# Side jobs dealt anew over eight slots, q computed once and its halves exchanged by transfers, v taken from k's job

## The chip, the core and the metric

The kernel runs on one core of one Trainium2 chip. The time is the device time of one execution in microseconds (us). TensorE is called PE in the profile, VectorE DVE, ScalarE ACT, GpSimd POOL, SyncE SP (SPq is its queue, which issues the transfers here).

## What is computed

A block of a transformer on x of shape (16, 512, 128), all in float32:

```python
xn = layernorm(x)
# attention, 16 heads of 8, 4 kv heads
q = (xn @ Wqa @ Wqb).reshape(b, s, 16, 8)
kv = (xn @ Wkva @ Wkvb).reshape(b, s, 4, 8, 2)
k, v = kv[..., 0], kv[..., 1]
q, k = rope(q), rope(k)          # pairs (2i, 2i+1) of a head's 8 numbers are rotated
k, v = repeat(k, 4), repeat(v, 4)
w = softmax(causal(q @ k.T * 8 ** -0.5))
attn = (w @ v) @ Wout + bout
# feed-forward with blocks of 16 quantized to FP4, 352 hidden
gate, up = fp4_linear(xn, w_gate), fp4_linear(xn, w_up)
ffn = fp4_linear(silu(gate) * up, w_down)
out = x + attn + ffn
```

## The kernel before

The work is a software pipeline over the 16 batches. Iteration T runs from -3 to 16; `Step.has(off)` says whether batch T+off exists. In iteration T the kernel computes the exponentials and weighted sums of batch T, the row maxima of batch T+1, the hidden layer's gate and up of T+1, the projections q, k, v and the quantization of xn of T+2, the statistics and normalization of x of T+3, and normalizes and stores the output of T-1.

An iteration has 8 slots (one for each pair of heads). On TensorE a slot is, in program order (`iteration`, L1125): six `max_tile` (scores for the maxima, three PSUM banks `max_ps`) and five `exp_tile` (scores for the exponentials, two banks `exp_ps`) in turn, with side jobs at three points: point 0 after exp tile 1, point 1 after exp tile 3, point 2 after max tile 5, and then `weighted_sums`, half of a kv head (L1057). The table `MISC` (L56) gives the side jobs of each slot and point as (job, bank, batch offset). A side job writes one of the two banks `misc_ps`, and waits until the bank's previous job has been read (`misc_wait`). Jobs: gate/up f (matmuls of token tile f), xnT, xqT, onT, ot0, ot1, hqT (transposes of normalized x, quantized x, normalized output, sums, quantized hidden layer), q and qrot (the projection and the same with each pair's columns swapped), kk (k and swapped k, four column groups each), v, mrow (the rows of maxima), out0 and out1.

Each engine carries out its own list in order. ScalarE (L968): after each exp its side read (th, up_half, the copies of the transposes) and `extra`: casts of q, k, x_mag (slot 0), h_mag (`H_POWERS`, L67), `normalize_x` in slot 5. VectorE (L715): six `reduce_tile` in a slot (the maxima, L662) with its own jobs between them: q_cos, q_sin, k_cos, k_sin, `gated`, `hidden_max`, `normalize`, `magnitudes`, `output`. GpSimd (L525): `causal` (masks P, four instructions for a kv head), `quantize` parts 0 to 3 of h and xq, `hidden`, q_rope, k_rope and their splits, the statistics. SP (L410): the transfers; `place_max` waits for ScalarE's m_row and puts the maxima's rows into Q; q_split and k_split go to scratch in DRAM and come back as Q and K.

Rope before is `q_rope = q_cos + q_sin`, q_cos from the q job and q_sin from the qrot job, each times a table.

Of the kernel before, what the change touches and what calls it, by code (L numbers as in the profile page):

```python
# [9 lines left out]
ALU = mybir.AluOpType  # L10
# [24 lines left out]
WRITE_Q, WRITE_K = 3, NT  # L35
LOAD_K, LOAD_Q, COPY_K = 6, 2, 2
# [88 lines left out]
def build(nc, x, wqaT, wkvaT, wqb, wkvb, wout, bout, wgate, wup, wdown, cosq, sinq, cosk, sink,  # L125
          mask_q, mask_k, out):
    ctx = ExitStack()
    with ctx:
# [46 lines left out]
        q_sin = sb("q_sin", [128, S])  # L175
        q_rope = sb("q_rope", [128, S])
# [6 lines left out]
        k_split = sb("k_split", [128, 3, 128], BF16)  # L183
        v_stage = sb("v_stage", [128, NT, KVH * D])
# [61 lines left out]
        xn_done = sem("xn_done")  # L246
        q_pool = sem("q_pool")
# [65 lines left out]
        def _(sp):  # L313
            sp.dma_start(x_in[:, :, :], x[0].rearrange("(c p) e -> p c e", p=128)).then_inc(x_loaded, 16)
            for dst, src in (
                (wqaT_sb[:, :], wqaT), (wkvaT_sb[:, :], wkvaT), (wqb_sb[:, :], wqb), (wkvb_sb[:, :], wkvb),
            ):
                sp.dma_start(dst, src).then_inc(factors_in, 16)
            for dst, src in (
                (cosq_sb[:, :], cosq), (sinq_sb[:, :], sinq), (cosk_sb[:, :], cosk), (sink_sb[:, :], sink),  # L320
            ):
                sp.dma_start(dst, src).then_inc(tables_in, 16)
# [24 lines left out]
            for half in range(2):  # L347
                r = HALF * half + MROW
                for i in range(2):
# [5 lines left out]
                    dst = bass.AP(tensor=q_scr[i].tensor, offset=NSLOT * E * S + half * D * NPAIR * S,  # L355
                                  ap=[[NPAIR * S, D], [128, NPAIR * NT], [1, 128]])
# [97 lines left out]
        def _(pool):  # L454
# [70 lines left out]
            def iteration(T):  # L525
# [6 lines left out]
                split_rest(T, 0, 1)  # L532
                hidden(T, 0)
# [7 lines left out]
                if T.has(0):  # L541
                    quantize(T, 0, 0, *hs)
# [13 lines left out]
                if T.has(2):  # L556
                    T.misc_wait(pool, misc_read, "q")
                    T.misc_wait(pool, misc_read, "qrot")
                    nc.gpsimd.tensor_tensor(q_rope[:, :], q_cos[:, :], q_sin[:, :], ALU.add).then_inc(q_pool, 1)
                    T.wait(pool, k_muls, 1, 2, 1)  # L560
                    T.misc_wait(pool, misc_read, "kk")
# [44 lines left out]
        def _(dve):  # L606
# [80 lines left out]
            def normalize(T, off, g):  # L687
# [27 lines left out]
            def iteration(T):  # L715
# [4 lines left out]

                reduces(0, 0, 1)
# [7 lines left out]
                reduces(0, 4)  # L729
                if T.has(2):  # L730
                    T.wait(dve, x_powers, 1, 2, 1)
                    magnitudes(lambda s, n: T.wait(dve, s, 2, 2, n), x_mag[:, :], x_mags)
                reduces(0, 5)
                first = T.t0 == FIRST_T + 1
                if first:
                    weight_scales()

                reduces(1, 0, 1)
                if T.has(2):
# [12 lines left out]
                reduces(2, 0, 1, 2)  # L752
                if T.has(2):
                    T.misc_wait(dve, misc_filled, "qrot")
                    nc.vector.tensor_tensor(q_sin[:, :], misc_ps[1][:, :], sinq_sb[:, :], ALU.mult).then_inc(misc_read[1], 1)
                reduces(2, 3)
                hidden_max(T, 1)
                reduces(2, 4)
                if T.has(2):

                    T.wait(dve, k_pool, 3, 1, 1)
                    T.misc_wait(dve, misc_filled, "kk")
                    nc.vector.tensor_tensor(k_cos[:, :], misc_ps[0][:, 0:128], cosk_sb[:, :], ALU.mult).then_inc(k_muls, 1)
                    nc.vector.tensor_tensor(k_sin[:, :], misc_ps[0][:, 128:256], sink_sb[:, :], ALU.mult).then_inc(misc_read[0], 1)
                reduces(2, 5)
# [5 lines left out]
                normalize(T, -1, 1)  # L771
                reduces(3, 1)
                if T.has(3):
                    T.wait(dve, x_loaded, 16, 3, 16)

                    T.wait(dve, var_done, 2, 2, 2)
# [4 lines left out]
                reduces(3, 3)
                if T.has(3):
                    for c in range(NT):
                        T.wait(dve, bn_done, NT, 3, c + 1)
                        dve.sem_inc(dve_marks, 1)
                        nc.vector.bn_aggr(bn_mv[:, c, :], bn_raw[:, c, :]).then_inc(mv_done, 1)
                reduces(3, 4)
# [8 lines left out]
                if T.has(0):  # L796
                    T.wait(dve, h_powers, NT, 0, NT)
                    magnitudes(lambda s, n: T.wait(dve, s, 2, 0, n), h_mag[:, :], h_mags)
                reduces(4, 1, 2)
# [22 lines left out]
                reduces(6, 3)  # L822
                reduces(6, 4, 5)
# [396 lines left out]
```

## Time and profile before

| | before |
|---|---|
| median of 3 runs | 816.93 us (815.31 to 818.28) |
| profiled execution | 814.38 us, of which the span from first to last instruction is 812.6 us |
| PE busy | 742.4 us, 91% of the span |
| DVE busy | 636.3 us, 78% |
| POOL busy | 606.1 us, 75% |
| ACT busy | 554.2 us, 68% |
| mean granted clock of TensorE | 0.985 |

Busy time is what an engine spends in instructions; a slot's time is read off as the distance of two starts. "x4" after a line of the timeline means four instructions merged, and "[0.27 <-DVE ...]" idle time before them and who ended it. A matmul's shown end lies a little behind the start of the next one, as they are pipelined. Some matmul records are missing from the trace.

### The profile page before, as it was taken

What the parts mean: (1) busy time and instruction counts of PE and PEld (TensorE: products, weight loads), DVE (VectorE), ACT (ScalarE), POOL (GpSimd) and SP (SyncE); (2) the same over time, 40 slices, a digit from 0 to 9 for tenths busy, and PEclk for the clock granted to TensorE, in tenths of its full rate; (3) what the DMA queues carried; (4) which work ended last, traced back from release to release, by engine and by line L of the source; (5) the groups of instructions that cost most, each with busy time, mean ns of one, the idle gap of its engine ahead of it and who ended that gap; (6) DMA issues with size and microseconds to landing.
All of it is one profiled execution on the core that took longest, in us unless ns stands there. A gap on an engine that the chain in (4) does not pass through costs nothing.

```text
span 812.6 us, 18664 instructions
## 1 busy us (share of the span) xinstructions
PE 742.4 (91%) x6641; PEld 465.3 (57%) x6733; DVE 636.3 (78%) x1394; ACT 554.2 (68%) x1170; POOL 606.1 (75%) x707
## 2 busy tenths in 40 slices
PE   2376999999999999999999999999999999999986
PEld 1233555665656566665656566665656566665544
DVE  5569888888788888888788888888788888877511
ACT  1212677777777777777777777777777777677672
POOL 5533697878788797878788797878788797856662
PEclk9977899999999999999999999999999999999999
DMA  4423232141414233241414232141414232240000
GB/s 113 122 55 103 55 97 59 57 114 47 100 33 111 54 97 73 66 105 46 101 34 110 55 103 68 57 114 46 102 35 107 54 94 63 59 99 3 28 8 20
DMA packets 66518, 58.24 MB, mean 72 GB/s; under 512 B 17554, under 2 KB 56434, under 8 KB 66426
## 3 DMA queue, kind: packets, MB, share of 16 engines
q1 hardware_dynamic: 66426, 57.04, 27.4%
q8 instruction: 54, 0.88, 0.5%
q14 instruction: 38, 0.31, 0.1%
HBM read 31.81 MB, written 18.61 MB: 62 GB/s over the span
## 4 chain that ended last, share of the span: by engine, by line
PE 73%; DVE 8%; ACT 6%; POOL 5%; issue 3%; SPq 2%; DMA 2%; another core or an unknown queue 0%; POOLq 0%; DVEq 0%; ACTq 0%
PE pv_ps L1057 18%; PE max_ps L1021 12%; PE exp_ps L1036 11%; PE misc_ps L1073 6%; PE max_ps L1022 6%; PE misc_ps L1122 5%; DVE neg_max L662 4%; PE misc_ps L1081 3%; PE misc_ps L1100 3%; ACT P L854 2%; PE misc_ps L1120 2%; PE misc_ps L1110 2%; PE misc_ps L1090 1%; POOL P L478 1%; PE misc_ps L1077 1%
## 5 line engine op out<-in xcount | busy, mean ns | idle before, releaser
L662 DVE TENSOR_REDUCE neg_max<-max_ps 128x1 f32<-128x512 f32 (+3 forms) x768 | 433.4, 594 | 110.3 <-PE max_ps L1022 108.7
L854 ACT ACTIVATE P<-exp_ps 128x512 f32<-128x512 f32 x512 | 293.5, 596 | 176.8 <-remote 95.7
L1021 PE MATMUL max_ps<-K,Q 128*128 128x384 bf16 (+2 forms) x768 | 199.7, 279 | 24.6 <-DMA Kd<-K 10.9
L1036 PE MATMUL exp_ps<-Q,K 128*128 128x384 bf16 (+3 forms) x932 | 208.4, 292 | 7.5 <-ACT P L854 6.0
L1022 PE MATMUL max_ps<-Kd,Q 128*128 128x128 bf16 x1024 | 190.7, 221 | 1.5 <-DVE neg_max L662 1.5
L478 POOL TENSOR_SCALAR_AFFINE_SELECT P<-P 128x512 f32<-128x512 f32 x256 | 161.6, 667 | 32.6 <-ACT P L857 32.6
L1057 PE MATMUL pv_ps<-P,V 128*32 128x512 f32 (+3 forms) x2048 | 164.2, 439 | 1.2 <-POOL P L478 0.8
L1021 PEld LDWEIGHTS max_ps<-K,Q 128*128 128x128 bf16 x768 | 75.2, 100 | 96.0 <-DVE neg_max L662 42.7
L1022 PEld LDWEIGHTS max_ps<-Kd,Q 128*128 128x128 bf16 x1024 | 99.4, 99 | 42.6 <-issue 22.8
L510 POOL TENSOR_TENSOR h<-gate_sb,up_half 128x352 f32<-128x352 f32 x64 | 59.6, 932 | 62.4 <-DVE gate_sb L675 62.3
L1036 PEld LDWEIGHTS exp_ps<-Q,K 128*128 128x128 bf16 x1024 | 82.3, 98 | 37.0 <-ACT P L854 14.2
L1057 PEld LDWEIGHTS pv_ps<-P,V 128*32 128x32 f32 x2048 | 53.7, 109 | 80.5 <-issue 70.8
L1073 PE MATMUL misc_ps<-wguT,xqT 128*128 128x352 f32 x256 | 94.0, 481 | 3.9 <-DVE o_norm L698 3.7
L857 ACT ACTIVATE P<-exp_ps 128x512 f32<-128x512 f32 x128 | 77.6, 606 | 0.4 <-PE exp_ps L1036 0.4
L1073 PEld LDWEIGHTS misc_ps<-wguT,xqT 128*128 128x128 f32 x256 | 47.0, 195 | 26.3 <-DVE o_norm L698 11.6
L1122 PE MATMUL misc_ps<-wdT,hqT 128*128 128x128 f32 (+1 forms) x384 | 53.3, 275 | 0.0
L1122 PEld LDWEIGHTS misc_ps<-wdT,hqT 128*128 128x128 f32 (+1 forms) x384 | 48.0, 192 | 0.0
L491 POOL TENSOR_TENSOR h<-h,h_mag 128x1408 f32<-128x1408 f32 x16 | 45.9, 2868 | 1.3
L488 POOL TENSOR_TENSOR h<-h,h_mag 128x1408 f32<-128x1408 f32 x16 | 45.8, 2862 | 0.0
L485 POOL TENSOR_TENSOR h<-h,h_inv 128x1408 f32<-128x1408 f32 x16 | 41.4, 2590 | 0.0
L494 POOL TENSOR_TENSOR h<-h,h_scale 128x1408 f32<-128x1408 f32 x16 | 41.4, 2589 | 0.0
L924 ACT ACTIVATE xn<-x_in,shift,rstd 128x128 f32<-128x128 f32 x64 | 30.5, 487 | 15.2 <-POOL shift L523 15.2
(113 smaller groups left out, 1024.0 us busy)
## 6 DMA issues: line engine op xcount, KB each, us to landing
Q<-q_scr SPq DMA_DIRECT2D x64, 224.0 KB
q_scr<-q_split SPq DMA_DIRECT2D x16, 384.0 KB, 2.6
Kd<-K SPq DMA_DIRECT2D x64, 96.0 KB
x_in<-x SPq DMA_DIRECT2D x16, 256.0 KB, 5.3
q_scr<-q_split SPq DMA_DIRECT2D x16, 256.0 KB, 2.9
x_res<-x SPq DMA_DIRECT2D x16, 256.0 KB, 5.8
out<-y SPq DMA_DIRECT2D x32, 128.0 KB, 3.1
K<-k_scr SPq DMA_DIRECT2D x64, 48.0 KB
```

The source lines that it names most:

```text
L478: nc.gpsimd.affine_select(out=diag, in_=diag, compare_op=ALU.is_ge, fill=0.0, base=0, pattern=[[0, GH], [1, 128]], channel_multiplier=-1). ...
L491: nc.gpsimd.tensor_tensor(t, t, mag[:, :], ALU.subtract).then_inc(quant, 1)
L510: nc.gpsimd.tensor_tensor(h[T.par(1)][:, f * F:(f + 1) * F], gate_sb[f % 2][:, :], up_half[f % 2][:, :], ALU.mult).then_inc(h_made, 1)
L662: nc.vector.tensor_reduce(neg_max[:, pr // 4, i, heads[0]:heads[0] + len(heads), pr % 4], max_ps[r % 3][:, 0:len(heads) * n].rearrange("p ...
L854: nc.scalar.activation(P[g % 2][:, hh + r % 2, col:col + 512], ps[:, :], ACT.Exp, scale=SCALE).then_inc(exp_done, 1)
L857: nc.scalar.activation(P[g % 2][:, hh:hh + 2, P_COL[2]:P_COL[2] + 256], ps[:, :].rearrange("p (h q) -> p h q", h=2), ACT.Exp, scale=SCALE) ...
L1021: nc.tensor.matmul(ps[:, col:col + d], Qt, Kt[:, half, g, 0:d], start=True, stop=True)
L1022: last = nc.tensor.matmul(ps[:, col + d:col + n], Qt, Kd[:, half, g, d:n], start=True, stop=True)
L1036: last = nc.tensor.matmul(exp_ps[n % 2][:, col:col + width], K[par][:, half, pr // 2, kb * 128:(kb + 1) * 128], Q[par][:, pr, kb * 128:S], ...
L1057: last = nc.tensor.matmul(pv_ps[32 * j:32 * j + 32, kb * 128:S], V[T.par(off)][:, kb, g, :], P[g % 2][:, j, P_COL[kb]:P_COL[kb] + width], ...
L1073: last = nc.tensor.matmul(ps[:, 0:F], xqT[T.par(1)][:, tok[f]], wguT[:, int(job[0] == "u"), :], start=True, stop=True)
L1122: last = nc.tensor.matmul(ps[:, tok[n]], hqT[0:cn, k, tok[c]], wdT[0:cn, k, :], start=False, stop=(k == 2))
```

## The change

Side jobs. The new table (with the batch offsets as in the old one):

```python
MISC = [
    [[("gate0", 0, 1), ("up0", 1, 1)], [], [("q", 1, 2)]],
    [[], [("gate1", 0, 1), ("up1", 1, 1)], [("ot0", 1, -1)]],
    [[("mrow1", 0, 0)], [], [("ot1", 1, -1), ("kkv", 0, 2)]],
    [[("gate2", 0, 1), ("up2", 1, 1)], [("v", 1, 2)], [("xqT", 0, 2)]],
    [[("gate3", 0, 1), ("up3", 1, 1)], [("onT", 1, -1)], []],
    [[], [("out0", 0, -1)], []],
    [[("out1", 0, -1)], [("mrow0", 1, 1)], []],
    [[("xnT", 1, 3)], [("hqT0", 0, 0), ("hqT1", 1, 0)], [("hqT2", 0, 0)]],
]
H_POWERS = [(1, 0), (1, 1), (1, 2), (2, 2)]
```

xnT moves from slot 0 to slot 7 of the iteration before, ot0 (and the division of its sums) from slot 7 to slots 1 and 2 of the next iteration, xqT from slot 5 to 3, three h_mag casts of ScalarE to slot 1 and one to slot 2.

q: qrot is gone. The tables and q are laid out by dimension (16 rows for each of the 8 numbers), VectorE makes q_cos and q_sin both from the q job, eight transfers of 16 rows exchange q_sin's pairs, and GpSimd subtracts:

```diff
+            def swap_q(T):
+                T.misc_wait(sp, misc_read, "q")
+                T.wait(sp, q_pool, 3, 1, 1)
+                for d in range(D):
+                    r, o = H * d, H * (d ^ 1)
+                    sp.dma_start(q_swap[r:r + H, :], q_sin[o:o + H, :]).then_inc(q_swapped, 16)
...
                     sp.dma_start(x_res[:, :, :], x[T.batch(0)].rearrange("(c p) e -> p c e", p=128)).then_inc(x_res_loaded, 16)
+                if T.has(2):
+                    swap_q(T)
+                if T.has(0):
                     place_max(T, 0, 1)
...
-                    nc.gpsimd.tensor_tensor(q_rope[:, :], q_cos[:, :], q_sin[:, :], ALU.add).then_inc(q_pool, 1)
+                    T.wait(pool, q_muls, 1, 2, 1)
+                    T.wait(pool, q_swapped, 16 * SWAP_Q, 2, 16 * SWAP_Q)
+                    nc.gpsimd.tensor_tensor(q_rope[:, :], q_cos[:, :], q_swap[:, :], ALU.subtract).then_inc(q_pool, 1)
```

v: it is computed transposed as a third set of the k job, copied to SBUF by VectorE, and transposed back:

```diff
-                elif job == "kk":
-                    for n in range(2):
-                        w = proj[:, 2 * E + n * KVH * D:2 * E + (n + 1) * KVH * D]
+                elif job == "kkv":
+                    for n in range(3):
+                        w = proj[:, E + n * KVH * D:E + (n + 1) * KVH * D]
                         for c in range(NT):
                             last = nc.tensor.matmul(ps[32 * c:32 * c + 32, n * 128:(n + 1) * 128], w, xnT[:, tok[c]], start=True, stop=True)
                 elif job == "v":
-                    for c in range(NT):
-                        last = nc.tensor.matmul(ps[:, 32 * c:32 * c + 32], xnT[:, tok[c]],
-                                                proj[:, 2 * E + 2 * KVH * D:], start=True, stop=True)
+                    T.misc_wait(pe, misc_read, "kkv")
+                    last = nc.tensor.transpose(ps[:, 0:128], vT[:, :], ident[:, :])
```

GpSimd: part 0 of h's quantization goes ahead of hidden(0), part 3 ahead of causal(2). VectorE's list in the new order, by slot (r0 to r5 are the reductions):

```
0: r0 r1 scales(h) r2 r3 gated0 r4 r5 q_cos
1: r0 q_sin r1 magnitudes(x) r2 r3 r4 gated1 r5
2: r0 normalize0 r1 r2 r3 r4 r5 normalize1 k_cos k_sin vT
3: r0 magnitudes(h) r1 r2 gated2 r3 r4 v_stage r5
4: r0 bn_stats r1 bn_aggr r2 gated3 r3 r4 r5
5: r0 r1 hidden_max0 r2 r3 hidden_max1 r4 output0 r5
6: r0 r1 x_max r2 output1 r3 hidden_max2 r4 r5
7: r0 r1 scales(x) r2 r3 hidden_max3 r4 r5
```

## Rows read from the trace of the kernel before

**Rows 1.** Busy time by stretch (T=7): length, PE, PEld, DVE, ACT, POOL, clock, DMA, GB/s

```profile
401.46:447.16 45.70, 44.87 (x418) 28.69 (x421) 38.72 (x86) 34.30 (x73) 37.48 (x44) 1.00 0.29 76
```

**Rows 2.** Timeline of TensorE, T=7: start us, us, engine, line, operation, tiles, count

```profile
404.59 0.66 PE L1077 MATMUL misc_ps<-ident,xn 128*128 128x128 f32 x4
...
406.95 0.34 PE L1021 MATMUL max_ps<-K,Q 128*128 128x384 bf16 x1
...
407.82 1.02 PE L1081 MATMUL misc_ps<-xnT,proj 128*128 128x512 f32 x2
408.68 0.27 PE L1021 MATMUL max_ps<-K,Q 128*128 128x256 bf16 x1
...
412.55 0.34 PE L1021 MATMUL max_ps<-K,Q 128*128 128x384 bf16 x1
...
415.67 0.64 PE L1087 MATMUL misc_ps<-xnT,proj 128*32 128x128 f32 x16
...
418.56 0.34 PE L1021 MATMUL max_ps<-K,Q 128*128 128x384 bf16 x1
...
421.92 1.03 PE L1090 MATMUL misc_ps<-proj,xnT 128*128 128x32 f32 x8
...
424.65 0.34 PE L1021 MATMUL max_ps<-K,Q 128*128 128x384 bf16 x1
...
428.21 0.23 PE L1021 MATMUL max_ps<-K,Q 128*128 128x128 bf16 x1
...
430.11 0.34 PE L1021 MATMUL max_ps<-K,Q 128*128 128x384 bf16 x1
...
435.90 0.34 PE L1021 MATMUL max_ps<-K,Q 128*128 128x384 bf16 x1
```

**Rows 3.** Timeline of TensorE, T=14, slots 0 to 2

```profile
721.11 0.34 PE L1021 MATMUL max_ps<-K,Q 128*128 128x384 bf16 x1
...
724.41 0.39 PE L1036 MATMUL exp_ps<-Q,K 128*128 128x256 bf16 x2
...
726.06 0.34 PE L1021 MATMUL max_ps<-K,Q 128*128 128x384 bf16 x1
...
727.35 0.39 PE L1036 MATMUL exp_ps<-Q,K 128*128 128x384 bf16 x2
...
729.96 1.28 PE L1057 MATMUL pv_ps<-P,V 128*32 128x384 f32 x16
731.17 0.34 PE L1021 MATMUL max_ps<-K,Q 128*128 128x384 bf16 x1
...
736.46 0.34 PE L1021 MATMUL max_ps<-K,Q 128*128 128x384 bf16 x1
```

**Rows 4.** Timeline of ScalarE, T=7, slots 0 and 2

```profile
404.06 0.47 ACT L893 ACTIVATE up_half<-misc_ps 128x352 f32<-128x352 f32 x1
404.41 1.10 ACT L854 ACTIVATE P<-exp_ps 128x512 f32<-128x512 f32 x2
...
415.88 0.49 ACT L965 ACTIVATE h_mag<-h 128x352 bf16<-128x352 f32 x1
```

**Rows 5.** Timeline of VectorE, T=7, slot 4

```profile
428.54 0.51 DVE L675 SCALAR_TENSOR_TENSOR gate_sb<-th,misc_ps 128x352 f32<-128x352 f32 x1
```

**Rows 6.** Timeline of SP's queue, T=7: start us, us, line, transfer, count

```profile
415.24 2.56 SPq L408 DMA_DIRECT2D Q<-m_row  x4
```

**Rows 7.** Transfers by line: count, KB each, median us from issue to landing

```profile
q_scr<-q_split SPq DMA_DIRECT2D x16, 384.0 KB, 2.6
...
k_scr<-k_split SPq DMA_DIRECT2D x64, 24.0 KB, 1.6
```

**Rows 8.** Timeline of all engines in the fill, T=-2 and the start of T=-1

```profile
22.64 1.26 POOL L559 TENSOR_TENSOR q_rope<-q_cos,q_sin 128x512 f32<-128x512 f32 x1 [0.46 <-DVE q_sin L755]
...
25.13 0.41 SPq L439 DMA_DIRECT2D x_in<-x  x1
...
43.96 0.48 PE L1021 MATMUL max_ps<-K,Q 128*128 128x384 bf16 x1 [8.88 <-DMA Kd<-K]
```

More of the change, by code:

```diff
@@ L532, in iteration @@
                 split_rest(T, 0, 1)
+                if T.has(0):
+                    quantize(T, 0, 0, *hs)
                 hidden(T, 0)
@@ L728, in iteration @@
                 gated(T, 0)
[L729 to L734, printed above, removed]
+                reduces(0, 4, 5)
                 if first:
                     weight_scales()
-                reduces(1, 0, 1)
                 if T.has(2):
@@ L770, in iteration @@
                 reduces(3, 0)
[L771 to L776, printed above, removed]
-                    for c in range(NT):
-                        nc.vector.bn_stats(bn_raw[:, c, :], x_in[:, c, :]).then_inc(bn_done, 1)
-                reduces(3, 2)
-                gated(T, 2)
[L781 to L787, printed above, removed]
+                if T.has(0):
+                    T.wait(dve, h_powers, NT, 0, NT)
+                    magnitudes(lambda s, n: T.wait(dve, s, 2, 0, n), h_mag[:, :], h_mags)
+                reduces(3, 1, 2)
+                gated(T, 2)
+                reduces(3, 3, 4)
                 if T.has(2):
@@ L795, in iteration @@
                 reduces(4, 0)
[L796 to L799, printed above, removed]
+                if T.has(3):
+                    T.wait(dve, x_loaded, 16, 3, 16)
+                    T.wait(dve, var_done, 2, 2, 2)
+                    for c in range(NT):
+                        nc.vector.bn_stats(bn_raw[:, c, :], x_in[:, c, :]).then_inc(bn_done, 1)
+                reduces(4, 1)
+                if T.has(3):
+                    for c in range(NT):
+                        T.wait(dve, bn_done, NT, 3, c + 1)
+                        dve.sem_inc(dve_marks, 1)
+                        nc.vector.bn_aggr(bn_mv[:, c, :], bn_raw[:, c, :]).then_inc(mv_done, 1)
+                reduces(4, 2)
                 gated(T, 3)
-                reduces(4, 3)
-                hidden_max(T, 2)
-                reduces(4, 4, 5)
+                reduces(4, 3, 4, 5)
                 if first:
                     store_weights()
-                reduces(5, 0, 1, 2)
+                reduces(5, 0, 1)
+                hidden_max(T, 0)
+                reduces(5, 2, 3)
+                hidden_max(T, 1)
+                reduces(5, 4)
                 output(T, 0)
-                reduces(5, 3, 4)
-                hidden_max(T, 3)
                 reduces(5, 5)
@@ L1074, in misc_job @@
                 elif job == "xnT":
-                    T.wait(pe, xn_done, NT, 2, NT)
+                    T.wait(pe, xn_done, NT, off, NT)
                     for c in range(NT):
                         last = nc.tensor.transpose(ps[:, tok[c]], xn[:, c, :], ident[:, :])
-                elif job in ("q", "qrot"):
-                    T.misc_wait(pe, misc_read, "xnT")
-                    c0 = E * int(job == "qrot")
-                    last = nc.tensor.matmul(ps[:, :], proj[:, c0:c0 + E], xnT[:, :], start=True, stop=True)
-                elif job == "kk":
-                    for n in range(2):
-                        w = proj[:, 2 * E + n * KVH * D:2 * E + (n + 1) * KVH * D]
+                elif job == "q":
+                    T.prev().misc_wait(pe, misc_read, "xnT")
+                    last = nc.tensor.matmul(ps[:, :], proj[:, 0:E], xnT[:, :], start=True, stop=True)
+                elif job == "kkv":
+                    for n in range(3):
+                        w = proj[:, E + n * KVH * D:E + (n + 1) * KVH * D]
                         for c in range(NT):
```

101 lines of the change are left out of this document (53 added, 48 removed), and 6 rows, old and new, of the table MISC.

## Prediction

> **What bounds the kernel now.** I read the busy time by stretch first. One iteration T handles the attention of batch T, the maxima of T+1 and the projections of T+2. In T=7, TensorE is busy 44.87 of 45.70 us at its full clock (granted clock 1.00, the 2.4 GHz level), VectorE 38.72, ScalarE 34.30, GpSimd 37.48 [rows 1]. The timeline of TensorE gives the slots: each starts with the first `max_tile` matmul, so T=7, from 401.46 to 447.16, has slots of 5.49, 5.60, 6.01, 6.09, 5.46 and 5.79 us, and 11.26 for slots 6 and 7 together [rows 1, 2]. T=14 starts at 721.11 [rows 3]; the seven iterations from 401.46 take 45.66 each, so the loop is regular and what one iteration gains or loses counts some 15 times.
>
> But TensorE's queue is in order, and it stands still as soon as the next tile has no bank. Three couplings matter. An exp tile n+2 needs exp tile n read by ScalarE (two banks). A max tile n+3 needs n reduced by VectorE. A side job needs the previous job of its misc bank read. So the question for each slot is what fills TensorE while ScalarE works, not only what TensorE has to do.
>
> T=14 shows that: it has no batch T+2, so xnT, q, qrot, kk, v are absent. Its slot 1 has nothing at point 0, as in the new plan. It lasts 5.11 us (726.06 to 731.17), where 5.60 less the q job (0.86, from 407.82 to 408.68) would be 4.74: exp tile 2 starts only 1.29 us after the slot's start [rows 2, 3]. Of 0.86 us taken off, 0.37 came back as waiting.
>
> **Matmul work.** Removed per iteration: qrot, like q 0.86; v 1.03 less the 0.16 by which a shown end lies behind the next start, 0.87. Added: a third set of four matmuls in kkv, half of the 0.57 that kk takes (0.64 less overlap), 0.29; and one transpose of vT (four take 0.66 less 0.17 = 0.49 after a wait; I take 0.44 for four without one, an estimate), a quarter of that and some start, 0.17 [rows 2]. Net -1.27.
>
> **Slots, one by one, in the new plan** (S is the slot's start).
>
> Slot 0 (gate0/up0; q at point 2). T=14's slot 0, without xnT, is 4.95. There exp tile 4 starts at S+3.30 [rows 3]. In T=7 ScalarE also casts x_mag, so its third exp starts at S+2.95, ends at S+3.55 [rows 4], and TensorE can follow 0.06 later, at S+3.61 (the 0.06: up_half starts at 404.06 and lasts 0.47, xnT starts at 404.59 [rows 2, 4]). xnT used to fill that time; q now comes behind it. 4.95 + 0.31 + 0.86 = 6.12 (before 5.49).
>
> Slot 1 (nothing; gate1/up1; ot0). Base 5.11. Three h_mag casts move here, each 0.49 long; ScalarE's instructions overlap by 0.1, so two exps take 1.10 and not 1.20, and a cast costs 0.39 [rows 4]. ScalarE: first exp at S+0.64, then four exp steps of 0.49, three casts of 0.39, th 0.35, up_half 0.46, some 0.04 less in all by the overlaps: bank 1 free at S+4.54, TensorE at S+4.60. In T=14 the weighted sums start at S+3.90 [rows 3], with 0.10 of weight load before them, so ot0 could have started at S+3.80. 5.11 + 0.80 + 0.49 (four transposes after such a wait) = 6.40 (5.60). Were ScalarE not late it would be 5.55.
>
> Slot 2 (mrow1; nothing; ot1, kkv). T=14's slot 2 has just mrow1 and ot1 and lasts 5.29 [rows 3]. kkv adds 0.57 + 0.29 + 0.09 = 0.95: 6.24 (6.01).
>
> Slot 3 (gate2/up2; v; xqT). The h magnitudes (two VectorE instructions) move here from slot 4. In T=7's slot 4 they hold max tile 4 until S+3.56 (428.21), behind onT [rows 2]; now behind the small v job. xqT then waits until `gated` has read gate2: S+3.89 plus 0.51 is S+4.40 [rows 5]. 4.46 + 0.49 + 0.10 + 1.21 (the weighted sums, 729.96 to 731.17 [rows 3]) = 6.26 (6.09; the wait of up2 on `normalize` goes, since that is moved ahead of slot 3).
>
> Slot 4 (gate3/up3; onT) loses the magnitudes: 5.46 - 0.31 = 5.15 (an estimate: max tile 4 right behind onT instead of at 428.21). Slot 5 (nothing; out0) loses xqT, 0.44, and gets the wait of an empty point 0, 5.11 - 4.74 = 0.37, and a normalize_x between the exps that costs as an h_mag cast does, 0.39: 6.11 (5.79). Slots 6 and 7: xnT alone at point 0, the hqT jobs stay; 11.3 (11.26).
>
> Sum 6.12 + 6.40 + 6.24 + 6.26 + 5.15 + 6.11 + 11.3 = 47.58, against 45.70: **+1.85 us an iteration**, rounded. Bounds: +2.6 (GpSimd late in slot 6 by 0.5, slots 6 and 7 as much as slot 2) and +0.9 (ot0 finds its bank free, and slot 4 lends its 0.3 to slot 3).
>
> **GpSimd.** h part 3 goes ahead of causal(2), 2.6 us before it. h part 0 moves ahead of hidden(0): both have slack. Counting its chain from `gated` in slot 3, the first two of causal(2) end within 0.1 us of when TensorE wants them in slot 6. I take 0, bound 0.5. V and vT copies: VectorE gets 0.2 us more in 38.72 of 45.70, hidden at slot ends; uncovered it would be 0.2.
>
> **SP and the swap.** `swap_q` issues eight transfers, then `place_max(T, 0, 1)` waits behind it. Four transfers from `place_max` took 2.56 us to issue, so eight take 5.1; landings have medians of 1.6 (24 KB) and 2.6 (384 KB), so 2 for these 32 KB [rows 6, 7]. q_sin is there at S0+7.8, the last issue ends at S0+12.9, and the last landing is at about 15; q_rope comes up on GpSimd at S0+16.5, and its cast on ScalarE at S0+19.9. In the steady loop the swap is hidden, with some 4 us; uncovered, it would delay ScalarE in slot 3.
>
> In the fill it is not hidden. SP is held by the constants until 25.13, when it issues the x load of 0.41 [rows 8]; then come eight issues, 5.1, and 2 of landing: q_rope at 32.6 rather than 22.64 [rows 8]. Bounds: issues of 0.4 each give 30.8, landings of twice as long 34.6. GpSimd and ScalarE are in order, so k_rope, both splits and the cast of the weights are behind it, and the first max tile, which idled 8.88 us until 43.96 for its K [rows 8], moves with them. **+9.5 us** (+6 to +12).
>
> By the Trainium skill, *DMA: Bandwidth & Descriptors*, "Rules for kernel authors", transfers under 64 KB are mostly overhead and should be coalesced; these are 32 KB each. Its section on the anatomy of one DMA gives about 2.0 us fixed for one on another path; paid one after another, eight of them would be an estimated 16 us instead of 7. No row of before shows these transfers.
>
> **Ends.** T=0 as the loop, +1.8 (the ends are estimates by the same steps). T=14 has ot0 and the casts in slot 1 but less in slots 3, 4 and 7: +0.8. T=15 and T=16: +1.5.
>
> Sum: 812.6 of span + 1.8 around it = 814.4; + 9.5 + 1.8 + 13 x 1.85 (24.0) + 0.8 + 1.5 = 852.0. The median of before (816.9) is 2.5 above its profiled run, so some 854.
>
> **Rivals.**
> 1. *ScalarE late, fill longer* (forecast): 854, own range 841 to 868. For it: T=14. Chance 0.70.
> 2. *TensorE's work counts in full*: the waits are covered by other tiles; -1.27 x 16 = -20, fill +9.5: about 806. For it: 44.87 of 45.70 busy. Against: T=14's slot 1 saved 0.49 of 0.86. It decides if exp tile 2 starts before S+1.1 in the new slot 1. Chance 0.08.
> 3. *Half*: ot0 finds bank 1 free and slot 3's waits overlap (+0.9 down to 0), or the fill moves by 3 only: 822 to 841. Chance 0.13.
> 4. *The swap lands late in the loop*: eight transfers one after another put q_rope at S0+24, 4 us behind its place, some 2 to 4 us of TensorE per iteration: 880 to 915. The 2 us each are my landing estimate of above. (It is the Trainium skill's rule, *DMA: Bandwidth & Descriptors*, "Rules for kernel authors", as a mechanism of this kernel.) Against: SP idles ahead of q_sin, and transfers overlap elsewhere. Chance 0.07. An outcome within 0.3% of before (about what a measurement of this kernel can tell from no change) needs a gain in the loop that just cancels the fill: 0.02.
>
> Range 832 to 870: the forecast's range, half of rival 3 and the unknown bounds. Faster 0.08, same 0.02, slower 0.90.
>
> **What would show it.** After: slots of about 6.1, 6.4, 6.2, 6.3, 5.15, 6.1; TensorE idle by "ACT P" (exp) in slots 0, 1, 2, 5; ot0 starting 0.06 after up_half in slot 1; the first max tile near 53 us; q_rope never idle on its transfer in the loop. It is wrong if slot 1 stays below 5.7, if the first max tile stays near 44, or if TensorE waits in slot 6 for GpSimd by more than 0.5.

## The result, and the profile after

The changed kernel takes 836.81 us (median, 836.56 to 837.29); the kernel before, run on the same chip beside it, 816.84 (815.31 to 818.28). The ratio is 1.0248, 95% interval 1.0225 to 1.0270: slower, as forecast, but by 20 us and not by 37.

| | before | after |
|---|---|---|
| span of the profiled execution | 812.6 us | 835.6 us |
| PE busy | 742.4 us, 91% | 738.6 us, 88% |
| DVE busy | 636.3 us, 78% | 621.6 us, 74% |
| POOL busy | 606.1 us, 75% | 600.0 us, 72% |
| ACT busy | 554.2 us, 68% | 544.8 us, 65% |
| first max tile starts | 43.96 | 50.66 |
| an iteration of the loop (T=7) | 45.70 | 46.81 |

Every engine has less to do and the kernel is slower. Below, "before" is the kernel before and "after" the changed one; the fill is the stretch up to T=0, in which the pipeline is not yet full. The busy time by stretch, for the eight slots of T=7 in the kernel after (columns as in [rows 1]), with the sum of the iteration last:

```profile
413.02:419.19 6.17, 5.77 (x48) 3.08 (x45) 5.33 (x11) 3.99 (x9) 5.05 (x6) 1.00 0.52 151
419.19:425.61 6.42, 5.75 (x50) 3.13 (x47) 4.76 (x10) 4.41 (x10) 3.58 (x5) 1.00 0.21 52
425.61:431.56 5.95, 5.39 (x75) 3.20 (x71) 5.21 (x13) 3.83 (x8) 5.18 (x10) 1.00 0.08 18
431.56:437.35 5.79, 5.64 (x52) 3.31 (x48) 4.74 (x10) 4.97 (x11) 3.87 (x5) 1.00 0.00 0
437.35:442.49 5.14, 5.14 (x51) 3.26 (x48) 4.61 (x15) 4.17 (x10) 4.82 (x12) 1.00 0.51 167
442.49:448.59 6.10, 5.70 (x59) 3.82 (x56) 4.42 (x9) 4.18 (x9) 6.02 (x3) 1.00 0.33 88
448.59:454.31 5.72, 5.72 (x63) 4.10 (x59) 4.58 (x9) 3.59 (x7) 5.64 (x7) 1.00 0.48 133
454.31:459.83 5.52, 5.46 (x59) 3.78 (x55) 4.20 (x11) 4.49 (x9) 2.86 (x4) 1.00 0.18 48
sum 46.81, PE 44.57 PEld 27.69 DVE 37.86 ACT 33.63 POOL 37.02; mean PE 5.57 PEld 3.46 DVE 4.73 ACT 4.20 POOL 4.63
```

It answers [rows 1]: the gap between an iteration's length and PE's busy time was 0.83 us before and is 2.24 now, and it lies in slots 0, 1, 2 and 5. (Before, the eight slots were 5.49, 5.60, 6.01, 6.09, 5.46, 5.79, 5.72 and 5.54, read from the starts of their first max tiles; the same slot differs by up to 0.02 from one iteration to the next. About six matmul records an iteration are missing before, x932 against x1024 in the rows below, so its gap is, if anything, read too large.) The groups of the costliest instructions say who ended the idle time, first of after, then of before (busy, mean ns | idle before, releaser):

```profile
L1056 PE MATMUL exp_ps<-Q,K 128*128 128x512 bf16 (+3 forms) x1024 | 244.0, 301 | 33.7 <-ACT P L877 28.0
```

```profile
L1036 PE MATMUL exp_ps<-Q,K 128*128 128x384 bf16 (+3 forms) x932 | 208.4, 292 | 7.5 <-ACT P L854 6.0 <-issue 0.6
```

Exp tiles waited 28.0 us in all for ScalarE to read their bank, against 6.0. The chain that ended last turned the same way, of after and then of before:

```profile
PE 54%; ACT 24%; issue 8%; DVE 5%; SPq 4%; POOL 3%; DMA 2%; ACTq 0%; POOLq 0%; DVEq 0%
```

```profile
PE 73%; DVE 8%; ACT 6%; POOL 5%; issue 3%; SPq 2%; DMA 2%; another core or an unknown queue 0%; POOLq 0%; DVEq 0%; ACTq 0%
```

Where it sat in the new slot 1, by the timelines of ScalarE and TensorE of after:

```profile
420.33 0.49 ACT L985 ACTIVATE h_mag<-h 128x352 bf16<-128x352 f32 x1
...
421.19 0.50 ACT L985 ACTIVATE h_mag<-h 128x352 bf16<-128x352 f32 x1
...
422.06 0.51 ACT L985 ACTIVATE h_mag<-h 128x352 bf16<-128x352 f32 x1
...
423.26 0.49 ACT L913 ACTIVATE up_half<-misc_ps 128x352 f32<-128x352 f32 x1
...
423.81 0.66 PE L1128 MATMUL misc_ps<-ident,oT 128*128 128x128 f32 x4 [0.26 <-ACT up_half L913]
```

Three casts stand ahead of up_half; it ends at 423.75, and ot0 starts 0.06 later.

The fill, by the timeline of the queue of SP, GpSimd and TensorE; it answers [rows 8]:

```profile
25.52 0.40 SPq L461 DMA_DIRECT2D x_in<-x  x1
25.96 5.02 SPq L427 DMA_DIRECT2D q_swap<-q_sin  x8
32.46 1.26 POOL L581 TENSOR_TENSOR q_rope<-q_cos,q_swap 128x512 f32<-128x512 f32 x1 [6.77 <-DMA q_swap<-q_sin]
...
44.91 0.73 SPq L396 DMA_DIRECT2D Q<-q_scr  x2
...
50.66 0.48 PE L1041 MATMUL max_ps<-K,Q 128*128 128x384 bf16 x1 [2.60 <-DMA Kd<-K]
```

The same load of Q, and the first max tile, in before:

```profile
35.07 1.66 SPq L385 DMA_DIRECT2D Q<-q_scr  x2
```

The swap came as forecast, and the 9.8 us it costs q_rope did not all reach the first max tile: 6.7 did. The two transfers that load Q took 0.73 us to issue instead of 1.66, which the forecast did not have.

### The profile page after: what moved, and what is told of

The parts are those of the page before. It is cut to its first block, busy times and chain, and to the rows that moved or that the text cites. A ratio compares the mean times of both kernels' runs of the same rounds, so it can differ in the third digit from the quotient of the medians.

```text
span 835.6 us, 18869 instructions
## 1 busy us (share of the span) xinstructions
PE 738.6 (88%) x6717; PEld 449.4 (54%) x6717; DVE 621.6 (74%) x1411; ACT 544.8 (65%) x1170; POOL 600.0 (72%) x707
## 4 chain that ended last, share of the span: by engine, by line
PE 54%; ACT 24%; issue 8%; DVE 5%; SPq 4%; POOL 3%; DMA 2%; ACTq 0%; POOLq 0%; DVEq 0%
PE pv_ps L1077 18%; ACT P L877 11%; PE exp_ps L1056 10%; PE max_ps L1041 6%; PE misc_ps L1140 5%; DVE neg_max L683 3%; PE max_ps L1042 3%; PE misc_ps L1093 3%; ACT up_half L913 2%; PE misc_ps L1128 2%; ACT h_mag L985 2%; PE misc_ps L1138 2%; ACT th L900 2%; PE misc_ps L1100 1%; PE misc_ps L1118 1%
## 5 line engine op out<-in xcount | busy, mean ns | idle before, releaser
L683 DVE TENSOR_REDUCE neg_max<-max_ps 128x1 f32<-128x512 f32 (+3 forms) x768 | 429.1, 593 | 137.1 <-PE max_ps L1042 136.9
L1056 PE MATMUL exp_ps<-Q,K 128*128 128x512 bf16 (+3 forms) x1024 | 244.0, 301 | 33.7 <-ACT P L877 28.0
L500 POOL TENSOR_SCALAR_AFFINE_SELECT P<-P 128x512 f32<-128x512 f32 x256 | 153.4, 635 | 37.4 <-ACT P L880 37.4
L1056 PEld LDWEIGHTS exp_ps<-Q,K 128*128 128x128 bf16 x1024 | 77.7, 98 | 86.0 <-ACT P L877 65.5
L1093 PE MATMUL misc_ps<-wguT,xqT 128*128 128x352 f32 x256 | 88.6, 469 | 0.4 <-DVE vT L786 0.4
L510 POOL TENSOR_TENSOR xq<-xq,x_mag 128x512 f32<-128x512 f32 x16 | 18.5, 1155 | 44.5 <-DVE x_mag L645 44.5
L620 POOL TENSOR_TENSOR xq<-xn,x_inv 128x512 f32<-128x512 f32 x16 | 16.9, 1058 | 37.3 <-DVE x_inv L636 37.3
```

The costliest lines, as they stand in the source:

```text
L500: nc.gpsimd.affine_select(out=diag, in_=diag, compare_op=ALU.is_ge, fill=0.0, base=0, pattern=[[0, GH], [1, 128]], channel_multiplier=-1). ...
L510: nc.gpsimd.tensor_tensor(t, t, mag[:, :], ALU.add).then_inc(quant, 1)
L683: nc.vector.tensor_reduce(neg_max[:, pr // 4, i, heads[0]:heads[0] + len(heads), pr % 4], max_ps[r % 3][:, 0:len(heads) * n].rearrange("p ...
L1056: last = nc.tensor.matmul(exp_ps[n % 2][:, col:col + width], K[par][:, half, pr // 2, kb * 128:(kb + 1) * 128], Q[par][:, pr, kb * 128:S], ...
L1093: last = nc.tensor.matmul(ps[:, 0:F], xqT[T.par(1)][:, tok[f]], wguT[:, int(job[0] == "u"), :], start=True, stop=True)
```

## The experiments

The theory: (A) TensorE loses where it waits for ScalarE with no side job to fill the wait, so what counts is where side jobs and casts stand. (B) The fill pays the swap. Against them: that the arithmetic itself (q once, v in k's job) costs, or that a transfer does. First I put the two pieces of arithmetic in the old deal (the old table of side jobs), together and apart. Each ratio is to the kernel before on the same chip; medians of runs on different chips are less comparable.

**Both in the old deal.** The deal, casts and orders are those of before; the jobs and the rope are those of after:

```diff
-    [[("mrow1", 0, 0), ("qrot", 1, 2)], [("kk", 0, 2)], [("ot1", 1, -1)]],
+    [[("mrow1", 0, 0)], [("kkv", 0, 2)], [("ot1", 1, -1)]],
```

> q once with the exchange, and v in k's job, but side jobs, casts and VectorE's and GpSimd's order as before. Theory A (the new deal of side jobs costs the time: ScalarE's waits at empty points and behind the casts): the loop gets shorter than before's 45.68 us, by about 0.5 in slot 2 and 0.4 in slot 3 less 0.2 of waiting for q_sin in slot 1, so 44.9 to 45.1 an iteration; the fill is 5 us longer; in all 808 to 813 profiled. Rival B (q once, the exchange and v in k are themselves what costs): the loop stays at 46.5 or above, 830 or more.

Measured: 820.46 us, ratio 1.0076 (1.0061 to 1.0092); first max tile at 50.35, iteration 45.83. Neither theory's number came: 44.9 to 45.1 had been expected by A, 46.5 or more by B. Slots 2, 3 and 4 are shorter (5.83, 5.65 and 5.31), but slot 1 is 5.90 and slot 7 is 6.14 instead of 5.54; the two runs below say why. Of the 20 us some 6 belong to the arithmetic and its fill, and the rest to the new deal, with the orders of VectorE and GpSimd that came with it. In the profiled execution, 7.9 longer than before's, T=1 starts 4.7 us later than before, T=1 to T=13 add 1.6, and the last stretch adds 1.6.

**q once alone**, without kkv and vT:

> Only q once with the exchange, deal as before. Theory A: loop 45.68 - 0.5 (qrot was partly cover for ScalarE in slot 2, of its 0.86 only 0.5 come back) + 0.2 (up1 waits until q_sin has read the bank) = 45.4; fill +5; in all 814 to 817 profiled, level with before. Rival B: loop 46 or more, 825 or more.

Measured: 820.72 us, ratio 1.0077 (1.0061 to 1.0094). First max tile at 49.89, iteration 45.57, a little more than the 45.4 expected, and a time 3 us above the 814 to 817 (T=1 starts 3.5 us later than before, the loop gives back 1.3; behind T=14 the profiled execution had a granted clock of 0.90 instead of 1.00 and took 3.5 longer). The product that left slot 2 gave 0.40 us there (6.01 to 5.61), but slot 1 grew by 0.30 (5.61 to 5.91): both q products are now made by VectorE from bank 1 ahead of up1. The timeline of VectorE and of TensorE in this kernel:

```profile
411.84 0.69 DVE L764 TENSOR_TENSOR q_cos<-misc_ps,cosq_sb 128x512 f32<-128x512 f32 x1 [0.29 <-PE misc_ps L1100]
412.45 0.68 DVE L767 TENSOR_TENSOR q_sin<-misc_ps,sinq_sb 128x512 f32<-128x512 f32 x1
```

```profile
412.34 1.71 PE L1093 MATMUL misc_ps<-wguT,xqT 128*128 128x352 f32 x4
```

The gate and up pair takes 1.71 us from start to end, against 1.40 in the same slot of after; up1 waits until q_sin has been made, at 413.13. Removing 0.86 us of matmuls per iteration bought 0.1.

**v in k's job alone**:

```diff
-                    for n in range(2):
+                    for n in range(3):
...
+                    nc.vector.tensor_copy(vT[:, :], misc_ps[0][:, 256:384]).then_inc(misc_read[0], 1)
...
+                    last = nc.tensor.transpose(ps[:, 0:128], vT[:, :], ident[:, :])
```

> Only v taken from k's job and transposed back, deal as before. Theory A: slot 2 +0.1, slot 3 -0.7 + 0.26 (exp tile 4 then waits for ScalarE), so loop -0.3 an iteration, no change in the fill: 808 to 811 profiled. Rival B (copy and transpose on the path): level or slower, 814 or more.

Measured: 819.60 us, ratio 1.0060 (1.0045 to 1.0075), iteration 45.89: a miss, since I had expected a gain. Slots 2, 3 and 4 went from 6.01, 6.09, 5.45 to 6.23, 5.65, 5.31, which is the gain I had expected (-0.36). Slot 7, where nothing had been touched, went from 5.53 to 6.11 and took more than that back, a net loss of 2.2 us from T=1 to T=14 (3.5 more lie behind T=14 in the profiled execution, again at a clock of 0.90 instead of 1.00). Its third transpose of h waits for `normalize` (L698), and `normalize` is late behind a tiny instruction. Timelines of this kernel, VectorE, GpSimd and TensorE:

```profile
398.58 0.84 DVE L611 TENSOR_SCALAR x_scale<-x_max 128x32 f32<-128x32 f32 x1
```

```profile
398.11 1.27 POOL L592 TENSOR_TENSOR x_bias<-x_res,bout_sb 128x512 f32<-128x512 f32 x1
```

```profile
401.26 0.64 PE L1102 MATMUL misc_ps<-ident,h 128*96 128x128 f32 x4 [0.44 <-DVE o_norm L698]
```

And the same pair in before:

```profile
443.25 0.27 DVE L611 TENSOR_SCALAR x_scale<-x_max 128x32 f32<-128x32 f32 x1
```

```profile
442.22 1.27 POOL L592 TENSOR_TENSOR x_bias<-x_res,bout_sb 128x512 f32<-128x512 f32 x1
```

The same 32 numbers a partition took 0.84 us here and 0.27 there. In both, x_scale ends 0.03 to 0.04 us after x_bias: 399.42 after 399.38, and 443.52 after 443.49. So x_scale seemed to be held until GpSimd's instruction had ended; with TensorE 0.4 us quicker in slots 2 to 4, VectorE came to it 0.6 us earlier in x_bias's run.

**x_bias moved.** To test that, GpSimd carries out x_bias behind the scaling of xq, its next instruction, instead of ahead of it; the rest is as in the run before.

```diff
-                    nc.gpsimd.tensor_tensor(x_bias[:, :, :], x_res[:, :, :],
...
                     nc.gpsimd.tensor_tensor(blocks(xq[:, :]), blocks(xn[:, :, :].rearrange("p c e -> p (c e)")),
...
+                    nc.gpsimd.tensor_tensor(x_bias[:, :, :], x_res[:, :, :],
```

> v in k's job alone (as in v_only), and on GpSimd x_bias is put behind the xq scaling instead of ahead of it. Theory: VectorE's small x_scale instruction (128x32) cannot end before the GpSimd instruction that runs when it starts; in v_only it took 0.84 us (398.58 to 399.42) because x_bias ran until 399.38, in before it took 0.27 because x_bias ended at 443.49. With x_bias behind xq it takes 0.17 to 0.28, normalize ends some 0.6 earlier, hqT2 has no wait, slot 7 goes from 6.11 to 5.53 and the iteration from 45.89 to about 45.3 us: 811 to 813 us in all, ratio 0.993 to 0.995 (v_only: 1.006). Rival A: x_scale is slow for a reason of its own and stays at 0.84: slot 7 stays at 6.1, time 819 to 820. Rival B: x_scale is short but GpSimd, whose x_bias now ends later, delays causal in slot 0 and the next x_res load: x_scale 0.2, but another slot longer, 815 to 819.

Measured: 811.03 us, ratio 0.9949 (0.9928 to 0.9970), iteration 45.26, slot 7 5.47, all other slots as they were. VectorE and GpSimd in this kernel:

```profile
440.87 0.17 DVE L611 TENSOR_SCALAR x_scale<-x_max 128x32 f32<-128x32 f32 x1
```

```profile
441.79 1.06 POOL L594 TENSOR_TENSOR xq<-xn,x_inv 128x512 f32<-128x512 f32 x1 [1.33 <-DVE x_inv L615]
442.80 1.28 POOL L599 TENSOR_TENSOR x_bias<-x_res,bout_sb 128x512 f32<-128x512 f32 x1
```

With nothing running on GpSimd x_scale takes 0.17. The theory named the instruction, the slot and the size beforehand, and both rivals fall. The Trainium skill, *SBUF — State Buffer*, "SBUF: two separate sides", says that VectorE in a two-port mode and GpSimd share a pair of ports under an exclusive lock: whoever starts first keeps it for its whole instruction and the other is blocked. The three durations agree; whether x_scale runs in such a mode no run here shows.

**q's rows by dimension alone.** The order of q's rows that the swap wanted (all heads of one dimension together, so that a dimension's step in the scratch is H*S), with qrot kept and no swap; the tables and `proj` are permuted to match.

```diff
-                                  ap=[[E * S, NSLOT + 1], [NPAIR * S, D], [1, NPAIR // 2 * S]])
+                                  ap=[[E * S, NSLOT + 1], [H * S, D], [1, NPAIR // 2 * S]])
```

> The kernel before with q's rows laid out by dimension (tables, projection columns, scratch), qrot kept. Theory C (rows by dimension let the two outer dimensions of the Q load fall together, which shortens its issue from 1.6 to 0.74 us and its landing, seen in after): first max tile of T=-1 at 40 to 41.5 instead of 43.96, landings of x_res near 3 us instead of 5.8, loop unchanged: 809 to 812 profiled. Rival D (the shorter fill stage in after has another cause, such as what else is queued then): first max tile stays at 43.5 to 44.5, time as before.

Measured: 808.62 us, ratio 0.9927 (0.9912 to 0.9942). The loop is that of before, 45.68; the first max tile starts at 40.68 instead of 43.96, and T=1 at 121.00 instead of 127.36, so the gain is 3.3 us at the first max tile and 6.4 by T=1. SP's queue and TensorE in this kernel:

```profile
35.23 0.74 SPq L389 DMA_DIRECT2D Q<-q_scr  x2
...
40.68 0.48 PE L1028 MATMUL max_ps<-K,Q 128*128 128x384 bf16 x1 [5.45 <-DMA Kd<-K]
```

The issue of the Q load took 0.74 us instead of 1.66. The transfers by line, first of before, then of this kernel (count, KB each, median us to landing):

```profile
x_in<-x SPq DMA_DIRECT2D x16, 256.0 KB, 5.3
...
x_res<-x SPq DMA_DIRECT2D x16, 256.0 KB, 5.8
```

```profile
x_in<-x SPq DMA_DIRECT2D x16, 256.0 KB, 3.1
...
x_res<-x SPq DMA_DIRECT2D x16, 256.0 KB, 3.1
```

Transfers that are issued behind the Q load land in 3.1 us instead of 5.3 and 5.8, though they themselves are unchanged.

**Padded.** In the changed kernel, one row of padding for each of the seven parts of the scratch (`(NSLOT + 1, E, S)` becomes `(NSLOT + 1, E + 1, S)`, and the outer step `E * S` becomes `(E + 1) * S`). The bytes and the rows' order are the same; only the outer step no longer equals eight inner ones.

> The changed kernel with one unused row between the slots of q's scratch, so that the outer dimensions of the Q load can't fall together; all else as in after. Theory C: issue of the two Q loads back to 1.6 us, Kd's landing to about 6.4, first max tile near 54 instead of 50.66, loop unchanged: 838 to 841 profiled. Rival D: no change.

Measured: 843.27 us, ratio 1.0313 (1.0292 to 1.0334), the iteration as in after (46.83), and this row in SP's queue:

```profile
44.92 1.70 SPq L396 DMA_DIRECT2D Q<-q_scr  x2
...
54.00 0.48 PE L1041 MATMUL max_ps<-K,Q 128*128 128x384 bf16 x1 [5.90 <-DMA Kd<-K]
```

The first max tile moved from 50.66 to 54.00, T=1 from 132.13 to 139.10, and x_in's landing back to 5.3; the profiled 843.07 are 2 us above the 838 to 841 expected. So what speeds up is the access pattern: with H*S inside E*S the two outer dimensions, 7 and 8, are one of 56 even steps. The Trainium skill, *DMA: Bandwidth & Descriptors*, "Why a DMA increments its semaphore by 16 and not by 1", says that a transfer runs on the largest number of engines, up to 16, that divides the slowest dimension of both its access patterns, and that each of them ends with its own write to the semaphore. By that rule it is 7 engines with an outer dimension of 7, and 14 with one of 56. The packets of the two executions bear it out, of after and then of the padded kernel:

```profile
DMA packets 71047, 62.42 MB, mean 75 GB/s; under 512 B 20034, under 2 KB 58914, under 8 KB 70954
```

```profile
DMA packets 70599, 62.42 MB, mean 74 GB/s; under 512 B 19586, under 2 KB 58466, under 8 KB 70506
```

The bytes and the larger packets are the same; after has 448 more of under 512 B, 7 for each of its 64 loads of Q. So the data is cut into the same pieces, and what differs is 7 more small packets a load, as 14 engines instead of 7 would write. Which engines carried the data the trace does not tell, and that their number is what halves the time is argued, not tested by itself.

**Casts late.** In the changed kernel, the h_mag casts stand behind exp tiles 3 and 4 of slots 1 and 2.

```diff
-H_POWERS = [(1, 0), (1, 1), (1, 2), (2, 2)]
+H_POWERS = [(1, 3), (1, 4), (2, 3), (2, 4)]
```

> The changed kernel with the four h_mag casts after exp tiles 3 and 4 of slots 1 and 2 instead of after 0, 1, 2 of slot 1 and 2 of slot 2. Theory A (the casts ahead of th1 and up_half1 hold exp tile 3 and ot0's bank): slot 1 falls from 6.42 to about 5.8, others unchanged, loop 46.2, in all 826 to 829 profiled. Rival E (slot 1's length comes from the empty point 0 alone, or from VectorE): slot 1 falls by 0.2 or less, 833 or more.

Measured: 828.43 us, ratio 1.0121 (1.0099 to 1.0143). Slot 1 fell from 6.42 to 5.77, the other slots stayed, and up_half ended before ot0 wanted its bank. This one line is 8 to 10 of the 20 us (the medians differ by 8.4, the ratios by 0.0127, and the stretch from T=1 to T=14 by 8.2); it is theory A's most direct evidence.

**First swap early.** The first swap's eight transfers are issued before SP waits for the constants.

> The changed kernel with the eight transfers for batch 0 issued before SP waits for the landing of the constants. Theory F (in the fill q_rope waits for SP): q_rope of T=-2 starts near 29.3 instead of 32.46, first max tile near 47.5 instead of 50.66, all later the same: 832 to 833 profiled. Rival G (landing of the exchange or the weights hold the fill): under 1 us of gain.

Measured: 833.79 us, ratio 1.0196 (1.0170 to 1.0223); the loop unchanged at 46.83, q_rope at 29.41 and the first max tile at 47.04, 3.6 earlier. That is theory B.

**Magnitudes back in slot 4.** In the changed kernel, `magnitudes` of h behind max tile 0 of slot 4, as before.

> The changed kernel with the magnitudes of h back behind the first reduction of slot 4, where GpSimd runs its masks, instead of slot 3, where it waits. Theory H (these two VectorE instructions take 0.52 + 0.53 us while GpSimd is idle and 0.99 + 0.84 while it computes): they take about 1.8 in all again, max tile 4 of slot 4 waits, slot 4 goes from 5.14 to about 5.45, slot 3 unchanged, in all 839 to 841 profiled. Rival I (their length depends on something else): they stay near 1.05 together, no change of the time.

Measured: 855.98 us, ratio 1.0461 (1.0441 to 1.0480), iteration 48.12: far more than I had expected. Slot 4 went from 5.14 to 6.11 and slot 6 from 5.72 to 6.04; slot 3 did not move. In their place in after (slot 3), GpSimd had nothing to do (VectorE, after):

```profile
432.59 0.52 DVE L643 TENSOR_SCALAR h_mag<-h_mag 128x1408 uint16<-128x1408 uint16 x1
433.14 0.53 DVE L645 TENSOR_SCALAR h_mag<-h_mag 128x1408 bf16<-128x1408 bf16 x1
```

In before the same two run beside GpSimd's `causal` (VectorE, then GpSimd):

```profile
425.69 0.99 DVE L622 TENSOR_SCALAR h_mag<-h_mag 128x1408 uint16<-128x1408 uint16 x1
426.72 0.84 DVE L624 TENSOR_SCALAR h_mag<-h_mag 128x1408 bf16<-128x1408 bf16 x1
```

```profile
425.08 2.97 POOL L478 TENSOR_SCALAR_AFFINE_SELECT P<-P 128x512 f32<-128x512 f32 x4
```

In the experiment they were slow again, beside `causal`, and in the new order the batch statistics come right behind them, ahead of the reads of max tiles 1 and 2 (VectorE of the experiment):

```profile
447.58 0.62 DVE L643 TENSOR_SCALAR h_mag<-h_mag 128x1408 uint16<-128x1408 uint16 x1
448.24 0.84 DVE L645 TENSOR_SCALAR h_mag<-h_mag 128x1408 bf16<-128x1408 bf16 x1
449.00 0.86 DVE L811 BATCH_NORM_STATS2 bn_raw<-x_in 128x6 f32<-128x128 f32 x4
449.78 0.67 DVE L683 TENSOR_REDUCE neg_max<-max_ps 128x1 f32<-128x512 f32 x1
```

That the two instructions are held by GpSimd fits x_scale's case, but no run separates it for them. The size I had missed since I had not counted the statistics. T=13 of the same execution bears that out: it has no batch T+3, so neither statistics nor what follows from them; its magnitudes are as slow (0.62 and 0.84), and its slots 4 and 6 last 5.14 and 5.72, as in after. So the slow magnitudes alone cost nothing there.

**The changed kernel, mended.** Casts late and first swap early as above, causal(2) back ahead of h part 3 on GpSimd, and q in slot 0 at point 1:

```diff
-    [[("gate0", 0, 1), ("up0", 1, 1)], [], [("q", 1, 2)]],
+    [[("gate0", 0, 1), ("up0", 1, 1)], [("q", 1, 2)], []],
```

> The changed kernel with four of its parts put back or mended: casts of the h magnitudes behind the exps of tiles 3 and 4, the first swap ahead of the constants' landing, causal(2) ahead of h part 3 on GpSimd, and q in slot 0 at point 1 instead of point 2. By my theory of waits a side job is free as far as it stands where TensorE waits for ScalarE: at point 1 q covers the wait of exp tile 4 that xnT covered in before, so slot 0 is 4.95 + 0.54 + 0.37 = 5.86 us instead of 6.18; slot 1 5.77, slot 6 of T=0 some 2.4 shorter than 8.27, first max tile near 47.0; iteration 45.85, span about 818 (814 to 822), ratio 1.000 to 1.008. By the rival that q counts in full wherever it stands, slot 0 stays at 6.18: iteration 46.2, span 822 to 825, ratio above 1.008.

Measured: 819.81 us, ratio 1.0054 (1.0039 to 1.0069), span 819.0. Slot 0 is 5.95 (6.18; 5.86 expected), slot 1 5.77, T=0's slot 6 4.79 instead of 8.27, the iteration 45.94, the first max tile at 47.84. So q costs 0.23 less at the point where ScalarE is waited for. What is left over before is not the fill: T=1 starts at 125.79, 1.6 us earlier than before's 127.36 (the first max tile is 3.9 later, but the faster load of Q helps). T=1 to T=13 add 2.8, and 5.2 lie behind the start of T=14, at a granted clock of 0.91 in the profiled execution's last stretch, where before had 1.00.

**A kernel faster than both.** From before: q's rows by dimension with qrot kept, v in k's job, x_bias behind xq.

> q's rows by dimension with qrot kept (by_dim_only), v in k's job, and x_bias behind xq. If the gains are of different places and add: fill as by_dim_only (first max tile near 40.7 us), iteration near 45.3 us, 806.3 - 14 x 0.37 = 801 us of span, median 802 to 805, ratio 0.982 to 0.986. If the shared cause of v_only's slot 7 is not x_bias: iteration 45.9, median about 811, ratio 0.995.

Measured: 804.27 us (802.57 to 806.66), ratio 0.9865 (0.9842 to 0.9889). First max tile at 40.31, and its T=7 by busy time:

```profile
391.62:436.88 45.26, 44.73 (x426) 28.12 (x422) 38.64 (x87) 34.24 (x73) 37.40 (x44) 1.00 0.28 77
```

The gains add (0.9927 x 0.9949 = 0.988): TensorE is busy 44.73 of 45.26 us.

## Why the prediction was right, and where it was off

The direction and the mechanism were right, the size was 17 us too large. The time lies below the forecast's own range of 841 to 868; the stated 832 to 870 holds it only because half of rival 3 had been added. Measured on the two profiled executions, the 23.0 us of span are: +6.7 at the first max tile, -1.7 in T=-1, -0.2 in T=0, +14.1 in T=1 to T=13, +4.1 from T=14 on. The forecast had 37.6 (9.5 up to the first max tile, 1.8 for T=0, 24.0 and 2.3). It was off by 14.6: 9.9 in the loop and 6.5 up to T=1, less 1.8 at the end. The other 2.5 are that I put the median 2.0 above the profiled execution, where it came out 0.5 below.

- *Slots 0, 1, 4, 5, and 6 with 7*: 6.12, 6.40, 5.15, 6.11, 11.3 forecast, 6.18, 6.42, 5.14, 6.10, 11.25 measured. Slots 0, 1 and 5 stood on T=14, where the empty point and its wait can be read. The row of up_half and ot0 above is the row that was named for slot 1, and the late casts took 0.65 of it away, where I had said 0.80 for ScalarE's lateness. In slot 5 normalize_x was put at 0.39; in T=13, which has no batch to normalize, the slot lasts 5.72, 0.38 less. Slot 4's number came, but its reason (the magnitudes go, -0.31) is not shown: in T=13 of the experiment that put them back, with 1.46 us of magnitudes in it and no statistics behind, it still lasts 5.14 (in before they take 1.83 us).
- *Slot 2, mis-sized term*: 6.24 forecast, 5.95 measured. I had summed 0.95 for kkv. From its first matmul to the weighted sums behind it there are 0.68 us in after:

```profile
429.68 0.86 PE L1106 MATMUL misc_ps<-xnT,proj 128*32 128x128 f32 x24
430.36 1.26 PE L1077 MATMUL pv_ps<-P,V 128*32 128x512 f32 x16
```

  I had 0.57 for two sets, 0.29 for the third and 0.09 for weight load. With a max tile behind it, as before, the group of three sets lasts 0.79 to 0.80 (v alone, 417.25 to 418.05), so the third costs 0.22, not 0.29; ahead of the weighted sums, which I had no row for, the same group gives way after 0.68, and the 0.09 is in it.
- *Slot 3, the step that failed*: 6.26 forecast, 5.79 measured. I took the h magnitudes to be as slow in their new place as in the old. They were 0.52 and 0.53 instead of 0.99 and 0.84, so `gated` came at S+3.09 and not at S+3.89 (the slot starts at 431.56), and xqT, at 435.59, did not have to wait for it:

```profile
434.65 0.51 DVE L696 SCALAR_TENSOR_TENSOR gate_sb<-th,misc_ps 128x352 f32<-128x352 f32 x1
...
437.34 0.34 PE L1041 MATMUL max_ps<-K,Q 128*128 128x384 bf16 x1
```

  With the magnitudes out of the slot altogether (the experiment above) it lasts 5.79 too; that magnitudes of 1.83 us would have made it 6.26 no run shows. Slots 2 and 3 together are 0.76 of the 0.77 us by which my iteration was too long, 10 us in the loop.
- *The fill, right but for a term put at nothing*: q_rope forecast at 32.6, measured at 32.46; eight issues 5.1 and 5.02; landing 2 and 1.9 (median). But the same change makes the load of Q faster. I had read the change of the access pattern in the diff as a renaming of rows, and did not cost it. The padded kernel has the swap without the faster load: its first max tile is 10.0 us later than before's, 9.5 forecast, and its T=1 11.7 us later (139.10 against 127.36), 11.3 forecast. In after T=1 is 4.8 us later; T=-1 is 1.7 shorter than in before, where it ends with a wait of 2.04 us for the copy of K, which after does not have. The faster load is thus worth 3.3 us at the first max tile and 6.4 (by dimension alone) to 7.0 (padded) by T=1. Part of the latter is the granted clock: padded's slots 6 and 7 of T=0 lasted 8.35 and 7.10 us at 0.82 and 0.73, after's 8.27 and 6.09, the latter at 0.89.
- *T=0*: +1.8 forecast, -0.2 measured, as two large differences cancel. Its slots 0 and 1 take 5.14 and 4.63 us in after, 7.05 and 5.06 in before, whose slot 0 waits 1.28 us for the maxima's rows and runs at a granted clock of 0.61 (0.98 in after). Its slot 6 takes 8.27 instead of 5.02: the weighted sums, at 123.80, wait for causal(2) behind h part 3, which starts at 122.47. Mended it starts at 117.17 and the slot lasts 4.79; with that order but late casts alone, or the early swap alone, it lasts 7.27. In the loop that order costs nothing, as forecast: the four instructions start at 451.68, the sums at 453.08, and TensorE is busy for the whole slot.
- *The ends*: +2.3 forecast, +4.1 measured. T=14's slots 0 to 6 are +0.7, near the 0.8 of the sum. From there to the end it is 57.4 us instead of 54.0, at a granted clock of 0.97 instead of 1.00; the padded kernel, with the same code there, takes 56.0 at 1.00. So some 1.4 of the 4.1 come with that execution's clock.

Rival 2 (matmuls count in full) fell where it said: slot 1 is 6.42, not under 5.7, its exp tile 2 starts at S+1.30 (420.49), not before S+1.1, and q once alone got 0.11 us an iteration for 0.86 of matmuls. Rival 4, with the Trainium skill's advice to coalesce, did not come: the eight transfers of 32 KB overlap, and q_rope waits for them twice, both times ahead of the loop (8.5 us in all, the second time at 66.37). No run has fewer and larger transfers for the swap, so what coalescing would give the fill is open. Rival 3's range (822 to 841) holds the measured time, and its reasons came in part: slot 3's wait was gone, though not by overlap, and the first max tile moved by 6.7, between its 3 and my 9.5. But ot0 did wait for its bank in full, and the fill did move by 9.8 up to q_rope.

## What to carry to other kernels

In an in-order queue a side job is worth its place more than its length: it costs less where the queue waits for another engine's bank (q 0.23 less of 0.86 here), so a removed or moved job must be costed from a stretch that already lacks it, as T=14 did here. Duration rows are only good for the neighbours they had: before carrying one to a new place, look at what GpSimd ran beside it. A change of layout is a change of every transfer's access pattern, and may be worth keeping when the change it came with is not.

## What the runs showed of the hardware

- A small VectorE instruction on SBUF operands that started while GpSimd ran one ended 0.03 to 0.04 us after it: 128x32 took 0.84 and 0.27 us beside a 1.27 us tensor_tensor of GpSimd's, and 0.17 with GpSimd idle. Moving that one GpSimd instruction behind its neighbour gave 0.63 us an iteration.
- A load of 224 KB whose two outer dimensions (7 and 8) have even steps issued in 0.37 us each instead of 0.83, and 256 KB transfers behind it landed in 3.1 us instead of 5.3 to 5.8. Each such load left 7 more packets of under 512 B, at the same bytes.
- Eight 32 KB transfers within SBUF from one queue took 0.62 to 0.78 us each to issue (4.95 in the loop, 5.02 and 6.20 in the fill), and landed 1.9 us after issue, overlapping.
- A third set of eight 32-column matmul records on a group of sixteen added 0.22 us ahead of a max tile (0.57 to 0.79); ahead of the weighted sums the same group took 0.68.
- The same code behind T=14's slot 6 took 56.0 us at a granted clock of 1.00 and 57.4 at 0.97.
